# Talking-heads attention on one core: softmax over two halves of the keys with a running maximum, a mixing matrix for each half, four score banks and a bank for the row work

## The reference, cut to what matters

```python
# x: (4, 2048, 256), 16 heads of 16
logits = einsum('bhid,bhjd->bhij', rope(q), rope(k)) * SCALE
logits = einsum('bhij,gh->bgij', logits, Wpre)        # mix over heads before the softmax
attn = softmax(logits, axis=-1)
attn = einsum('bhij,gh->bgij', attn, Wpost)           # and after it
out = einsum('bhij,bhjd->bhid', attn, v)
x = layernorm(x + out @ Wout.T + bout)
x = layernorm(x + soft_moe(x))                        # softmax dispatch and combine, 16 experts
```

## Time and profile before

| | us |
|---|---|
| median of 3 runs | 9455.35 (9444.43 to 9457.73) |
| the profiled execution | 9468.79 |
| its span in the profile | 9466.9 |
| mean granted TensorE clock | 0.975 of full speed |

### The profile page before, as it was taken

The page is one execution under the profiler, slowest core; times in us unless marked ns, Lnnn a source line. Parts: engine busy times, 40 slices in busy tenths (PEclk is TensorE's granted clock), DMA queues, the critical chain, the costliest instruction groups (busy, mean ns, idle before and its releaser), DMA issues.

```text
span 9466.9 us, 411153 instructions
## 1 busy us (share of the span) xinstructions
PE 8530.5 (90%) x158060; PEld 4596.5 (49%) x158060; DVE 8133.6 (86%) x16365; ACT 7179.3 (76%) x14720; POOL 5235.5 (55%) x8933
## 2 busy tenths in 40 slices
PE   7999999997799999999779999999978999999996
PEld 3545454544454544454445454545444544544444
DVE  7888988896789898889679888888967988898886
ACT  5887888885588788888558888888845888888884
POOL 5555655553555565555255555555525555555552
PEclk9999999998899999999899999999989999999998
DMA  0000000001000000000100000000020000000002
GB/s 29 7 9 8 8 7 8 8 7 66 20 7 8 8 8 7 9 7 7 66 21 7 8 8 8 7 9 8 8 69 16 7 8 8 9 7 8 7 9 73
DMA packets 101109, 144.57 MB, mean 15 GB/s; under 512 B 8096, under 2 KB 90656, under 8 KB 96800
## 3 DMA queue, kind: packets, MB, share of 16 engines
q1 hardware_dynamic: 99104, 117.57, 3.7%
HBM read 75.60 MB, written 41.94 MB: 12 GB/s over the span
## 4 chain that ended last, share of the span: by engine, by line
DVE 35%; PE 33%; issue 20%; ACT 7%; DVEq 2%; SPq 1%; DMA 1%; POOL 1%; ACTq 1%; POOLq 0%
PE psS L1177 16%; DVE mx L794 13%; DVE big L814 10%; PE psP L1197 7%; PE psO L1212 6%; DVE pl L845 5%; ACT pr L596 3%; ACT big L607 2%; PE psO L1223 1%; DVE top L798 1%; ACT rh L626 1%; PE psS L1316 1%; DVE rec L837 1%; PE psS L1151 1%; PE psS L1345 1%
## 5 line engine op out<-in xcount | busy, mean ns | idle before, releaser
L607 ACT ACTIVATE big<-psP 128x512 f16<-128x512 f32 x4096 | 2335.3, 595 | 1543.5 <-PE psP L1197 798.3
L814 DVE SCALAR_TENSOR_TENSOR big<-psP,big 128x512 f16<-128x512 f32 x4096 | 2650.0, 679 | 462.8 <-ACT big L607 459.4
L794 DVE TENSOR_REDUCE mx<-psS 128x1 f32<-128x512 f32 x4096 | 2718.4, 680 | 239.4 <-PE psS L1177 230.6
L1177 PE MATMUL psS<-KH,AH 128*128 128x512 f16 x8192 | 2478.0, 384 | 380.6 <-ACT pr L596 288.9
L596 ACT ACTIVATE pr<-psS,nmax 128x512 f32<-128x512 f32 (+1 forms) x3072 | 2527.7, 833 | 119.2 <-DVE nmax L805 104.5
L517 POOL TENSOR_TENSOR rl<-rp,rh 128x64 f16<-128x64 f32 x1024 | 811.7, 793 | 3115.3 <-issue 1823.7
L1177 PE MATMUL psS<-KH,AL 128*128 128x512 f16 x8192 | 2446.3, 380 | 0.0
L1177 PE MATMUL psS<-KL,AH 128*128 128x512 f16 x8192 | 2445.7, 380 | 0.0
L619 ACT ACTIVATE ph<-pr 128x512 f16<-128x512 f32 (+1 forms) x3072 | 2145.4, 772 | 0.1
L845 DVE TENSOR_TENSOR pl<-pr,ph 128x1024 f16<-128x1024 f32 (+1 forms) x2048 | 2003.9, 979 | 53.9 <-issue 26.0
L1197 PEld LDWEIGHTS psP<-rh,ph 64*128 64x128 f16 x32768 | 1433.7, 95 | 1106.8 <-DVE big L814 915.1
(11 more groups left out here) (136 smaller groups left out, 6195.1 us busy)
## 6 DMA issues: line engine op xcount, KB each, us to landing
ph<-in_xT SPq DMA_DIRECT2D x16, 512.0 KB, 4.5
xr<-in_x SPq DMA_DIRECT2D x64, 128.0 KB, 2.1
d_x<-x SPq DMA_DIRECT2D x64, 128.0 KB, 1.7
d_xn<-xn SPq DMA_DIRECT2D x64, 128.0 KB, 1.7
...
```

Of the source, the lines that this page charges most:

```text
L607: a.activation(PT[:, hf * JH:(hf + 1) * JH, :, 0, i0:i0 + HQ], psP[:, ih, :].rearrange("p (j g i) -> p j g i", j=JH, g=H), ACT.Copy, scale ...
L794: v.tensor_reduce(mx[:, t % 2, c:c + 1], psS[:, bank(t, c), :], X, ALU.max).then_inc(s_mx, 1)
L814: v.scalar_tensor_tensor(out=PT[:, js, :, 1, i0:i0 + HQ], in0=psP[:, ih, :].rearrange("p (j g i) -> p j g i", j=JH, g=H), scalar=MDROP, in ...
L1177: mm = pe.matmul(psS[:, bank(t, c), :], A_[:, k8, k, :], K_[:, k, c * CW:(c + 1) * CW], start=n == 0, stop=n == 5)
```

## The change

The keys are taken in two halves, h = 0 (chunks 0 and 1) and h = 1 (chunks 2 and 3). VectorE reduces each half with one instruction over 1024 columns (`half_max`), then takes the larger of the two (`row_bound`). ScalarE makes the bias of each half itself (`bound`: of half 0 from its own maximum, of half 1 from that of the row) and runs one exponential and one rounding (`highs`) over 1024 columns for each. The first half's probabilities are then too large by a factor that `factor` computes, f0 = exp(bias 1 - bias 0). It goes into the sum (`total`, now on GpSimd) and into the reciprocal of half 0 (`first_half`), so that rh and rl hold a matrix for each half; both are now made by GpSimd (`post`, `post_high`, `post_low`), and ScalarE's part of it is gone. psS has four banks, and psM gets a bank of its own; TensorE's waits that kept row work and outputs apart in the shared bank go. The order of each slot is new, and all four mixed_highs of ScalarE's slot are of tile T - 2. Scores of chunks 0 and 1 wait for the first exponential of the tile before, chunks 2 and 3 for the second.

The diff, cut to its core and with less indentation:

```diff
...
-rl = sb("rl", [P, 4, HP], F16)
+rh = sb("rh", [P, 4, 2, HP], F16)
+rl = sb("rl", [P, 4, 2, HP], F16)
 rt = sb("rt", [P, HP])
...
-psS = ctx.enter_context(nc.psum_tensor("psS", [P, NC + 1, CW], F32))
+psS = ctx.enter_context(nc.psum_tensor("psS", [P, NC, CW], F32))
 psP = ctx.enter_context(nc.psum_tensor("psP", [P, 2, CW], F32))
 psO = ctx.enter_context(nc.psum_tensor("psO", [P, CW], F32))
-psM = psO
-def bank(t, c):
-return NC if c == 0 and t % 2 else c
+psM = ctx.enter_context(nc.psum_tensor("psM", [P, CW], F32))
...
                         ALU.subtract).then_inc(s_plg, 1)
+    def total(T, t):
+        p = t % 2
+        g.wait_ge(s_exp, T * 2 + 2 + 1)
+        g.wait_ge(s_f, T + 1 + 1)
+        apart(g)
+        g.tensor_scalar(tot[:, p:p + 1], sums[:, p, 0:1], f0[:, p:p + 1], sums[:, p, 1:2],
+                        ALU.mult, ALU.add).then_inc(s_tot, 1)
+    def first_half(T, t):
+        p = t % 2
+        g.wait_ge(s_rec, T + 1 + 1)
+        g.tensor_tensor(rr[:, p, 0:1], rr[:, p, 1:2], f0[:, p:p + 1], ALU.mult).then_inc(s_r0, 1)
     def post(T, t):
-        g.wait_ge(s_rs, T * 2 + 2 + 1)
+        g.wait_ge(s_r0, T + 1 + 1)
         g.wait_ge(s_rl, T + 1)
         apart(g)
-        g.tensor_scalar(rp[:, :], rt[:, :], rec[:, t % 2:t % 2 + 1], None, ALU.mult).then_inc(s_rp, 1)
-    def post_low(T, t, early):
-        g.wait_ge(s_rp, T + 1)
-        g.wait_ge(s_rh, T + 1 + 1)
+        g.tensor_tensor(rp[:, :, :], rt[:, :].unsqueeze(1).broadcast_to([P, 2, HP]),
+                        rr[:, t % 2, :].unsqueeze(2).broadcast_to([P, 2, HP]), ALU.mult).then_inc(s_rp, 1)
+    def post_high(T, t, early):
+        g.wait_ge(s_rp, T + 1 + 1)
         if not early:
             g.wait_ge(s_D, (T - 3) * 2 + 1)
-        g.tensor_tensor(rl[:, t % 4, :], rp[:, :], rh[:, t % 4, :], ALU.subtract).then_inc(s_rl, 1)
+        apart(g)
+        g.tensor_copy(rh[:, t % 4, :, :], rp[:, :, :]).then_inc(s_rh, 1)
+    def post_low(T, t):
+        g.wait_ge(s_rh, T + 1 + 1)
+        g.tensor_tensor(rl[:, t % 4, :, :], rp[:, :, :], rh[:, t % 4, :, :],
+                        ALU.subtract).then_inc(s_rl, 1)
     def slot(it, t, first, work, live=True):
         T = (b * NIT + it) * TI + t
+        one = not (first and t < 1)
+        t_1 = (t - 1) % TI
+        if one:
+            total(T - 1, t_1)
         if live:
             mixq(it, t + LEAD, first and t + LEAD < TG)
         roots(t, work, 0)
+        if one:
+            low(T - 1, t_1, first and t < 3)
         if live:
             mixq_high(it, t + LEAD)
         roots(t, work, 1)
+        if one:
+            first_half(T - 1, t_1)
         if live:
             mixq_low(it, t + LEAD)
         roots(t, work, 2)
+        if one:
+            post(T - 1, t_1)
         if work is not None and t == POOL_SLOT["bias"]:
             add_bias(work)
-        if not (first and t < 1):
-            post(T - 1, (t - 1) % TI)
-            post_low(T - 1, (t - 1) % TI, first and t < 5)
-            low(T - 1, (t - 1) % TI, first and t < 3)
+        if one:
+            post_high(T - 1, t_1, first and t < 5)
         roots(t, work, 3)
+        if one:
+            post_low(T - 1, t_1)
     for t in range(LEAD):
         mixq(0, t, True)
...
     barrier(a, b * MEET + 2)
-    def exps(T, t, n, early):
-        c0, c1 = EXPS[n]
-        cs = slice(c0 * CW, c1 * CW)
-        if n == 0:
-            a.wait_ge(s_mx, T * 6 + 6 + 1)
-            if not early:
-                a.wait_ge(s_rs, (T - 1) * 2 + 1)
-                a.wait_ge(s_pl, (T - 1) * 2 + 1)
-                a.wait_ge(s_plg, T - 1 + 1)
-        s0 = bank(t, c0)
-        a.activation(pr[:, t % 2, cs], psS[:, s0:s0 + c1 - c0, :].rearrange("p c n -> p (c n)"), ACT.Exp,
-                     bias=nmax[:, t % 2:t % 2 + 1], scale=SSCALE,
-                     accum_out=sums[:, t % 2, n:n + 1]).then_inc(s_exp, 1)
+    def bound(T, t, h):
+        p = t % 2
+        m = 2 * h
+        a.wait_ge(s_mx, T * 3 + 2 * h + 1 + 1)
+        a.activation(nb[:, p, h:h + 1], top[:, p, m:m + 1], ACT.Copy, bias=LIFT * math.log(2.0),
+                     scale=-SSCALE).then_inc(s_nb, 1)
+    def exps(T, t, h, early):
+        p = t % 2
+        a.wait_ge(s_nb, T * 2 + h + 1 + 1)
+        if not early:
+            a.wait_ge(s_pl, (T - 2) * 2 + h + 1 + 1)
+            if h == 0:
+                a.wait_ge(s_tot, T - 2 + 1 + 1)
+            else:
+                a.wait_ge(s_plg, T - 2 + 1 + 1)
+        a.activation(pr[:, p, h * N2:(h + 1) * N2], psS[:, 2 * h:2 * h + 2, :].rearrange("p c n -> p (c n)"),
+                     ACT.Exp, bias=nb[:, p, h:h + 1], scale=SSCALE,
...
                      ACT.Copy, scale=MDROP).then_inc(s_mh, 1)
-    def highs(T, t, part, early):
-        cs = (slice(0, N2), slice(N2, NL), slice(NL, N))[part]
-        halves = (1, 2, 2)[part]
-        if part == 0:
-            a.wait_ge(s_exp, T * NE + NE + 1)
+    def highs(T, t, h, early):
+        cs = slice(h * N2, (h + 1) * N2)
+        a.wait_ge(s_exp, T * 2 + h + 1 + 1)
         if not early:
-            a.wait_ge(s_D, (T - 2) * 2 + halves + 1)
+            a.wait_ge(s_D, (T - 2) * 2 + h + 1 + 1)
         a.activation(ph[:, t % 2, cs], pr[:, t % 2, cs], ACT.Copy).then_inc(s_ph, 1)
-    def post_high(T, t, early):
-        a.wait_ge(s_rs, T * 2 + 2 + 1)
-        if not early:
-            a.wait_ge(s_D, (T - 3) * 2 + 1)
-        a.activation(rh[:, t % 4, :], rt[:, :], ACT.Copy, scale=rec[:, t % 2:t % 2 + 1]).then_inc(s_rh, 1)
...
         early = first and t < 2
-        def mixed(d, c):
-            if not (first and t < d):
-                mixed_high(T - d, (t - d) % TI, c, G + (t - d) // TG)
-        mixed(2, 2)
-        if not (first and t < 1):
-            post_high(T - 1, (t - 1) % TI, first and t < 5)
+        def mixed(c):
+            if not (first and t < 2):
+                mixed_high(T - 2, (t - 2) % TI, c, G + (t - 2) // TG)
+        mixed(0)
+        mixed(1)
         if live:
+            bound(T, t, 0)
             exps(T, t, 0, early)
-        mixed(2, 3)
+            highs(T, t, 0, early)
+        mixed(2)
+        mixed(3)
         if live:
+            bound(T, t, 1)
             exps(T, t, 1, early)
-            exps(T, t, 2, early)
-        mixed(1, 0)
+            factor(T, t, early)
+            highs(T, t, 1, early)
         if work is not None and t == ACT_SLOT["turn_u"]:
             turn(work)
-        mixed(1, 1)
         if work is not None and t == ACT_SLOT["weigh"]:
             weigh(work)
-        if live:
-            highs(T, t, 0, early)
-            highs(T, t, 1, early)
...
-    def chunk_max(T, t, c, early):
-        v.wait_ge(s_S, T * NC + c + 1)
-        if c == 0 and not early:
-            v.wait_ge(s_mx, (T - 1) * 6 + 1)
-        v.tensor_reduce(mx[:, t % 2, c:c + 1], psS[:, bank(t, c), :], X, ALU.max).then_inc(s_mx, 1)
+    def half_max(T, t, h):
+        v.wait_ge(s_S, T * NC + 2 * h + 2)
+        v.tensor_reduce(top[:, t % 2, h:h + 1], psS[:, 2 * h:2 * h + 2, :].rearrange("p c n -> p (c n)"),
+                        X, ALU.max).then_inc(s_mx, 1)
     def row_bound(T, t):
-        v.wait_ge(s_mx, T * 6 + 4 + 1)
-        v.tensor_reduce(top[:, 0:1], mx[:, t % 2, :], X, ALU.max).then_inc(s_mx, 1)
-    def shift(T, t, early):
-        v.wait_ge(s_mx, T * 6 + 5 + 1)
-        if not early:
-            v.wait_ge(s_exp, (T - 1) * NE + 1)
-        v.tensor_scalar(nmax[:, t % 2:t % 2 + 1], top[:, 0:1], -SSCALE, LIFT * math.log(2.0),
-                        ALU.mult, ALU.add).then_inc(s_mx, 1)
...
-    def total(T, t):
-        v.wait_ge(s_exp, T * NE + NE + 1)
-        v.tensor_reduce(tot[:, 0:1], sums[:, t % 2, :], X, ALU.add).then_inc(s_rs, 1)
-    def recip(T, t, early):
-        v.wait_ge(s_rs, T * 2 + 1 + 1)
-        if not early:
-            v.wait_ge(s_rl, T - 2 + 1 + 1)
-        v.reciprocal(rec[:, t % 2:t % 2 + 1], tot[:, 0:1]).then_inc(s_rs, 1)
...
         T = (b * NIT + it) * TI + t
         two = not (first and t < 2)
-        one = not (first and t < 1)
+        one = not (first and t < 1) and (live or t < 1)
         t_1, t_2 = (t - 1) % TI, (t - 2) % TI
-        if two:
-            low(T - 2, t_2, 1, first and t < 4)
         if live:
-            chunk_max(T, t, 0, first and t < 2)
+            half_max(T, t, 0)
         rows(t, work, 0)
-        if one:
-            total(T - 1, t_1)
         if t % TG == 3 and not (first and t < TG):
             out_copy((b * NIT + it) * 2 + t // TG - 1, (t // TG + 1) % 2, b * NIT + it - (1 if t < TG else 0))
-        if live:
-            chunk_max(T, t, 1, first and t < 2)
-        rows(t, work, 1)
-        if one:
-            recip(T - 1, t_1, first and t < 3)
         if two:
             mixed_low(T - 2, t_2, 0)
             mixed_low(T - 2, t_2, 1)
+        rows(t, work, 1)
+        if one:
+            low(T - 1, t_1, 1, first and t < 3)
+            recip(T - 1, t_1)
+        if live:
+            half_max(T, t, 1)
+            row_bound(T, t)
         rows(t, work, 2)
```

(73 more changed lines are left out.)

20 lines of the change are left out of this document (10 added, 10 removed).

## The result

The changed kernel takes 9100.66 us (median of 4 runs, 9096.98 to 9105.91) where the kernel before, in runs beside it, takes 9453.98: a ratio of 0.9628, 95% interval 0.9611 to 0.9645, so 3.7% faster. Forecast were 9215 us and a range of 9000 to 9510.

A forecast was written before the change was run, and what follows sets the result against it. No single engine: a loop through ScalarE and VectorE's row work held rows above TensorE's 124.2 us floor. 134.2 - 6.8 + 3.1 = 130.5 us a row, 3.7 less, times 64 = 240 us off: 9215 us, range 9000 to 9510.

The forecast's parts named there:

- what a row gains: Row of 16 tiles: from 134.2 to 130.5 us, 3.7 less, times 64 rows = 240 us.
- the ten microseconds: Row of 16 tiles: the loop's 134.2 us stand ten above TensorE's floor of 124.2, at most 640 us to win.
- ScalarE first copies the turn ..., and only then the first exponential: ScalarE's old order: copy and rh ahead of the first exponential make TensorE lose about 0.4 to 0.5 us a tile.
- the 0.37: Calm tiles: loss above TensorE's floor that the change removes, 0.37 us in each of 14, 5.2 us a row.
- some 2 us: VectorE's row work, ahead of the full row maximum: its share of a row's loss above TensorE's floor.
- ScalarE's sum: ScalarE's list per tile: 6.5 us busy plus 0.6 of gaps, 7.1 us, range 6.7 to 7.7; costs 1.4 a row.
- Rival 2: ScalarE takes the gain: 7.7 us a tile, 134 us a row, no change, 9440 us; chance 0.12.
- VectorE's sum: VectorE's list per tile: from 7.45 to 6.95 us, plus 0.3 of gaps; its bursts cost 1.7 us a row.
- rival 3: VectorE and GpSimd stop each other, operations held up to 1.2 us: slower, 136.5 us a row, 9600 us; chance 0.16.
- just fits: GpSimd's chain from reciprocal to rl: takes 2.4 us, with the reciprocal some 2.6 us ahead of the next T0.
- A row's Newton steps fill what is left: GpSimd: these steps use up the time remaining beside the 2.4 us chain to rl; no separate cost given.
- Banks: PSUM: chunk 0 losing its spare bank priced at nothing; the row bank's about 0.3 us a row not counted.

The follow-up runs named there:

- Experiment 2: Kernel before, with the first exponential moved ahead of the third copy and rh in ScalarE's slot: 9834 us, ratio 1.0393.
- experiment 4: Changed kernel with a second, unread copy of the one-element factor on ScalarE in each tile: 9123 us, ratio 0.964 to the kernel before.
- experiments 6 and 7: Changed kernel with each half maximum from two 512-wide reductions and a two-element maximum: two-input form 9676 us (1.0229), one-input form 9327 us (0.9865).
- experiment 7: Changed kernel with each half maximum from two 512-wide reductions, then a one-input reduction over two elements: 9327 us, ratio 0.9865 to the kernel before.
- experiment 3: Changed kernel with row work back in the outputs' bank and TensorE's waits restored: 9109 us, ratio 0.9627 to the kernel before.
- experiment 1: Changed kernel with the first half's bias also from the full row maximum, so both exponentials wait for it: 12158 us, ratio 1.2847.
- experiment 8: Changed kernel with the reciprocal ahead of row work and the 512-wide subtract in VectorE's slot: 9146 us, ratio 0.967 to the kernel before.

## Why the prediction was right, and where it wasn't

**The total** was in the range and on the right side; the gain was 3.7% where 2.5% was forecast. **The term of the sum that was mis-sized is what a row gains**: 3.7 us forecast, 5.7 measured, which is 366 us over 64 rows for the 240 of the sum. It was worked out on one row of 134.2 us, while the mean is 136.2. For that very row it holds: the reciprocals that answer to those of the earlier trace rows are

```profile
908.55 0.16 DVE L853 RECIPROCAL rr<-tot 128x1 f32<-128x1 f32 x1
...
1039.02 0.16 DVE L853 RECIPROCAL rr<-tot 128x1 f32<-128x1 f32 x1
```

so 130.5 us after. That the mean row after is 130.5 us too, as forecast to the tenth, is luck: the sum had the mean before too low and the gain too small by the same two microseconds.

**Where the ten microseconds go.** "ScalarE first copies the turn ..., and only then the first exponential" was in the main the wrong cause for a loss that is there. Experiment 2 shows that the full maximum came late on VectorE and that the copy stood mostly in idle time. In the tile of the earlier trace rows the exponential began at 1028.96, 0.14 us behind rh, and the bias had ended at 1028.77. I read the first and not the second. Nor is that tile a calm one: the reciprocals around it are at 1017.00, 1025.43 and 1033.97, 8.4 and 8.5 us apart, with a row's maxima on VectorE in between. The calm tile went from 7.36 to 7.00, TensorE's floor, so 0.36 a tile, as the sum had it, though its own rows give 7.36 - 7.04 = 0.32 for the 0.37. But most of the loss stood elsewhere. The sum gave VectorE's row work "some 2 us" of ten, and let 1.7 come back there. By the table the slots with the norms and the softmax stood 9.0 us above the floor before, of 12.0, and 4.5 after: the change took the most away where the sum saw a cost.

**ScalarE's sum.** "7.1 us a tile, a new near-bound": its list is 7.0 in calm tiles, busy time 6.9 where I said 6.5. The gaps were 0.03 and not 0.15, and the two errors are largely one: an instruction that depends on the one ahead also loses the overlap of 0.1, three times a tile, and that counts as busy time. As a bound the list is refuted by experiment 4, at least for 0.2 us. Rival 2 falls with it.

**VectorE's sum.** 6.95 forecast, 7.07 measured; the reduction at 1.21 was right. Its worth was undersold: my sum gave halves and order all of the gain, and VectorE's bursts a cost. By experiments 6 and 7 the shorter list is the larger part. The price of the list isn't linear: 0.2 us more cost 52 us over 1024 tiles, the 0.43 of experiment 7 (busy time 8101 for 7663 us) cost 224.

**GpSimd and rival 3.** Four more operations were free in throughput: 0.24 us of busy time a tile, not 1.0, since the old ones became shorter (at from 559 to 399 ns, rl from 793 ns for 64 columns to 428 for 128). The chain to rl "just fits" and in 180 cases didn't, 175 us of waits. "A row's Newton steps fill what is left" was the right place to look, and rival 3's mechanism is what it costs: for slots 8 and 12 of most rows a step is held by VectorE's subtract, and rl behind it comes 1.2 us too late. Rival 3 had this at 0.6 us a tile; it came twice a row, in 131 us of TensorE's waits. How much of them is lost time wasn't run. VectorE is hit for 33 ns a tile only (L827, 193 against 160 ns; some 0.7 us once a row), and the subtracts stayed at 1.223. With two more such instructions the form alone cost 344 us (experiments 6 and 7). GpSimd's own total took 639 ns where I said 0.2; it stood ahead of idle time.

**Banks.** Priced at nothing, measured at nothing (experiment 3). Chunk 0 without its spare bank leaves TensorE 1.3 us of waits for an exponential in all with halves; without them the kernel is 28% slower than the one before (experiment 1).

**Not foreseen:** the wait for ew at the end of tile 15. The change moved place 1 of row work behind two mixed lows and place 2 behind the second reduction, while TensorE had become earlier. I had said which waits the bank removes, but not what the new places do to the ones that stay.

Still open: the cause of experiment 8's loss, and what would be won by moving the Newton steps away from rl.
